# Side products of an attention and expert block on TensorE: full-array products in four groups a tile, against four column tiles of 32 in eight groups

## The reference

```
mod = silu(c) @ wmod            -> sa, ca, ga, sb, cb, gb per batch (ga, gb kept at 0.25 or more in size)
h  = layernorm(x) * (1 + ca) + sa
x  = x + ga * attention(h)      # 16 heads of width 8; head h has its own 64 rows of the batch
h  = layernorm(x) * (1 + cb) + sb
x  = x + gb * experts(h)        # router softmax over 8 experts, top 2, each expert a 128 x 128 matrix
```

## Time and profile before

| | us | share of span |
|---|---|---|
| profiled execution | 547.3 | |
| its span | 545.5 | |
| PE busy (4112 instructions) | 524.4 | 96% |
| PE weight loads | 221.6 | 41% |
| ScalarE busy | 495.6 | 91% |
| VectorE busy | 359.5 | 66% |
| POOL busy | 215.2 | 39% |
| exponentials L596, 512 of them | 485.8 | |
| weighted sums L795, 2048 matmuls | 247.8 | |
| scores L777, 1024 matmuls | 130.9 | |
| experts L825, 230 matmuls | 75.4 | |

### The profile page before, as it was taken

How to read it: one execution, slowest core, us unless ns; L and a number is a source line. 1 busy time by engine, 2 the same in 40 slices (tenths; PEclk the granted TensorE clock), 3 DMA queues, 4 the chain that set the end, 5 groups by cost and what they waited for, 6 DMA issues and landing times.

```text
span 545.5 us, 14324 instructions
## 1 busy us (share of the span) xinstructions
PE 524.4 (96%) x4112; PEld 221.6 (41%) x4112; DVE 359.5 (66%) x1259; ACT 495.6 (91%) x574; POOL 215.2 (39%) x430
## 2 busy tenths in 40 slices
PE   8789889999999999999999999999999999999897
PEld 8623334334343433434343434343333434343336
DVE  4446367667867666777766667867666677656466
ACT  1479999899999999999999999999999999999985
POOL 1223333344443344444333444443343444432344
PEclk9999999999999999999999999999999999999999
DMA  4663333333333333323333333233333332333000
GB/s 111 165 177 84 96 85 99 98 96 76 74 82 89 100 99 95 84 68 83 86 96 100 99 87 77 75 82 91 100 99 95 78 75 80 90 100 104 20 21 20
DMA packets 83341, 48.23 MB, mean 88 GB/s; under 512 B 59608, under 2 KB 74084, under 8 KB 83300
## 3 DMA queue, kind: packets, MB, share of 16 engines
q1 hardware_dynamic: 68860, 43.30, 29.7%
q10 hardware_dynamic: 14440, 4.38, 4.4%
HBM read 32.78 MB, written 14.87 MB: 87 GB/s over the span
## 4 chain that ended last, share of the span: by engine, by line
PE 88%; ACT 8%; issue 1%; DVE 1%; DMA 0%; SPq 0%; POOL 0%; DVEq 0%; POOLq 0%; ACTq 0%
PE ps_attn L795 43%; PE ps_scores L777 22%; ACT probs L596 8%; PE ps_side L825 8%; PE ps_side L715 3%; PE ps_side L722 2%; PE ps_side L731 1%; PE ps_side L709 1%; PE ps_side L808 1%; PE ps_scores L664 1%; PE ps_side L812 1%; PE ps_scores L825 1%; PE ps_side L702 1%; DMA wqkv_in<-in_L_attn_Wqkv_dram 0%; PE ps_attn L668 0%
## 5 line engine op out<-in xcount | busy, mean ns | idle before, releaser
L596 ACT ACTIVATE probs<-ps_scores 128x1024 f32<-128x1024 f32 x512 | 485.8, 1028 | 38.4 <-PE ps_scores L777 30.3
L795 PE MATMUL ps_attn<-probs,values 128*32 128x512 f32 x2048 | 247.8, 602 | 0.0
L777 PE MATMUL ps_scores<-query_stack,key_stack 32*128 32x512 f32 x1024 | 130.9, 500 | 15.1 <-ACT probs L596 8.7
L777 PEld LDWEIGHTS ps_scores<-query_stack,key_stack 32*128 32x128 f32 x1024 | 49.4, 183 | 166.1 <-ACT probs L596 161.2
L451 POOL TENSOR_SCALAR var_eps<-moments 128x1 f32<-128x1 f32 x64 | 12.4, 194 | 223.0 <-DVE moments L1167 151.0
L795 PEld LDWEIGHTS ps_attn<-probs,values 128*32 128x32 f32 x2048 | 53.6, 109 | 108.8 <-issue 108.7
L825 PE MATMUL ps_side<-experts_gated,h2T 128*128 (+1 forms) x230 | 75.4, 410 | 0.0
L1163 DVE TENSOR_TENSOR x<-ps_side,x_gated 128x128 f32<-128x128 f32 x31 | 9.0, 292 | 63.3 <-PE ps_side L825 59.1
L1156 DVE RECIPROCAL sums_inv<-sums 128x128 f32<-128x128 f32 x31 | 29.5, 952 | 27.7 <-DMA attnT<-a_scr 27.7
L1240 DVE TENSOR_TENSOR weighted<-ps_side,coef 128x256 f32<-128x256 f32 x114 | 46.5, 408 | 1.1 <-PE ps_side L825 1.1
L500 POOL TENSOR_TENSOR mix<-weighted 128x512 f32<-128x512 f32 x29 | 37.1, 1281 | 4.0 <-ACT weighted L614 4.0
(11 more groups left out here) (170 smaller groups left out, 514.1 us busy)
## 6 DMA issues: line engine op xcount, KB each, us to landing
key_stack<-k_scr SPq DMA_DIRECT2D x128, 128.0 KB, 2.7
query_stack<-q_scr SPq DMA_DIRECT2D x125, 64.0 KB, 2.2
q_scr<-qk_parts SPq DMA_DIRECT2D x94, 64.0 KB, 1.7
k_scr<-qk_parts SPq DMA_DIRECT2D x64, 64.0 KB, 1.7
a_scr<-attn ACTq DMA_DIRECT2D x120, 18.0 KB
sums<-a_scr SPq DMA_DIRECT2D x31, 64.0 KB, 2.1
attnT<-a_scr SPq DMA_DIRECT2D x31, 64.0 KB, 2.2
out_dram<-out_all ACTq DMA_DIRECT2D x28, 64.0 KB, 1.8
```

What stands on the lines that cost most here:

```text
L596: nc.scalar.activation(probs[:, k % RING, g, :], ps_scores[:, slot(k, g), :], ACT.Exp, scale=SCALE)\
L777: mm = nc.tensor.matmul(out_, key_stack[p0:p0 + 32, parity, 2 * k:2 * k + 2, :].rearrange("p j r -> p (j r)"), query_stack[p0:p0 + 32, par ...
L795: mm = nc.tensor.matmul(ps_attn[q:q + 32, :], values[:, parity, g, k, :], probs[:, k % RING, g, h * HALF:(h + 1) * HALF], start=(k == 0), ...
```

## The change

Every side product in the tiles is made by `product`: four matmuls with 32 weight columns each, on the four column tiles, over the same moving columns. The transposes are then ordinary products with the identity. The start-up and the end of the kernel keep the whole array.

TensorE's order becomes, for each key block k: scores of k, side group k, weighted sum of block k - 2. The four groups of experts are groups 1, 2, 5 and 7; a group waits for the emptying of the one before. VectorE's order follows. The experts are no longer gated ahead but the mix afterwards on POOL, except for the last batch (`experts_last`), and POOL copies the gated Wo of the batch to `wo_now`. The norm maximum becomes a flag for each row, and a product with ones counts the rows.

```diff
+            def product(dst, stationary, moving, whole):
+                if whole:
+                    return nc.tensor.matmul(dst, stationary, moving, start=True, stop=True)
+                for q in range(0, P, 32):
+                    mm = nc.tensor.matmul(dst[q:q + 32, :], stationary[:, q:q + 32], moving, start=True, stop=True, tile_position=(0, q))
+                return mm
+            def transposed(dst, src, whole):
+                return nc.tensor.transpose(dst, src, ident[:]) if whole else product(dst, src, ident[:], whole)
...
             def a_project_v(ps, u1, ring):
                 for n in range(G):
-                    for odd in range(2):
-                        mm = nc.tensor.matmul(ps[odd * R:(odd + 1) * R, n * R:(n + 1) * R],
...
+                    for q in range(0, P, 32):
+                        odd, r = q // R, n * R + q % R
+                        mm = nc.tensor.matmul(ps[q:q + 32, n * R:(n + 1) * R], hT[:, ring, r:r + 32],
+                                              wvT[:, odd].rearrange("p k d -> p (k d)"), start=True, stop=True, tile_position=(0, q))
...
-                nc.tensor.matmul(ps, norm_max[:].broadcast_to([P, P]), ident_r[:], start=True, stop=True).then_inc(ev["normT_done"], 1)
+            def a_flags(ps, u1):
+                reached(pe, ev["norm_flag_done"], u1)
+                nc.tensor.matmul(ps, ones_cols[:], norm_flag[:], start=True, stop=True, tile_position=(0, 0)).then_inc(ev["flags_done"], 1)
...
+            def side0(at, parity, before, after):
+                if before >= 4:
+                    reached(pe, weighted_done[1], at[-3])
...
+                if before >= 2:
+                    c_project(ps_side, at[-1])
                 if after >= 1:
+                    a_flags(ps_side[0:32, P + R:P + R + 1], at[2])
+            def emptied0(at, before, after):
+                if before >= 2:
+                    reached(pe, ev["x1_done"], at[-1])
                 if after >= 1:
+                    reached(pe, ev["bounded_done"], at[2])
+            def side1(at, parity, before, after):
+                if before >= 4:
+                    emptied0(at, before, after)
+                    c_experts(ps_side, experts_in, parity, 2)
+            def side2(at, parity, before, after):
+                if before >= 4:
                     reached(pe, weighted_done[2], at[-3])
+                    c_experts(ps_side, experts_in, parity, 3)
...
+            def side3(at, parity, before, after):
+                if before >= 4:
+                    reached(pe, weighted_done[3], at[-3])
...
+                    c_transpose(ps_side, at[-1])
                 if before >= 2 and after >= 1:
                     a_project_v(ps_side[:, P:2 * P], at[2], 1 - parity)
...
+            def side4(at, parity, before, after):
+                emptied3(at, before, after)      # h2T_done, values_done
                 if after >= 2:
                     a_project_qk(at[3], parity)
...
+            def side5(at, parity, before, after):
+                if before >= 3:
+                    emptied4(at, before, after)  # qkT_done
+                    c_experts(ps_side, experts_last if after == 0 else experts_in, 1 - parity, 0)
+            def side6(at, parity, before, after):
+                if before >= 3:
                     reached(pe, weighted_done[0], at[-2])
...
                 if after >= 3:
                     a_transpose(at[4])
+                if before >= 2 and after:
+                    c_logits(ps_side, at[-1], parity)
                 if after >= 2:
+                    a_norms(ps_side[:, P + NE:P + NE + 2 * J], at[3])
+            def side7(at, parity, before, after):
+                if before >= 3:
+                    if after >= 3:
+                        reached(pe, ev["hT_done"], at[4])
+                    if after >= 2:
+                        reached(pe, ev["norm_max_done"], at[3])
+                    if after:
+                        reached(pe, ev["logits0_done"], at[-1])
+                    c_experts(ps_side, experts_last if after == 0 else experts_in, 1 - parity, 1)
...
+                for k in range(KT):
                     with pe.If(flag == 0):
+                        if k == 0:
+                            exact_maxima(t, parity)
+                        scores(at[0], at[1], parity, k, True)
                     with pe.Else():
+                        if k == 0:
+                            pe.sem_inc(m_scores, M_PE)
+                        scores(at[0], at[1], parity, k, False)
...
+                    SIDES[k](at, parity, before, after)
+                    if k >= 2:
+                        weigh(at[0], at[1], parity, k - 2)
+                    elif before:
+                        weigh(at[-1], at[0], 1 - parity, KT - 2 + k)
```

Before, `c_weigh(.., 0)` stood directly behind `a_qk` and ahead of `a_qk_parts`, and `c_vals` ahead of `a_norm_max`. POOL's order: `gated_x` with the copy of Wo goes ahead of the `rstd` of the first norm, `mix_eight` behind the squares, and `mix_two` has one multiplication more:

```diff
+                g.tensor_tensor(mixed_gated[:], mixed[:], gate, ALU.mult).then_inc(ev["mixed_gated_done"], 1)
...
+                g.tensor_copy(wo_now[:], wo).then_inc(ev["wo_done"], 1)
```

More of the change, by code:

```diff
@@ L815, in c_experts @@
[L815 removed]
+                product(ps[:, P:P + NE], h2T[:, ring, :], routerT[:], whole).then_inc(ev["logits_done"], 1)
+            def c_experts(ps, weights, ring, piece, whole=False):
                 e0, e1 = PIECES[piece]
                 if piece == 0:
[L820 to L826 removed]
@@ L907, in side3, with tile @@
                 if after == 0:
-                    c_project(ps, at[0], (T - 2) // TB)
-            def counts(t, before):
+                    c_project(ps_side, at[0], wo_gated[:, (T - 2) // TB, :])
+            SIDES = (side0, side1, side2, side3, side4, side5, side6, side7)
+            def tile(t, parity, before, after):
                 at = {n: plus(pe, t, n) for n in range(-4, 5)}
-                batch = {n: batch_of(pe, at[-n]) for n in (2, 3, 4) if n <= before}
-                return at, batch
@@ L916, in between_sides @@
-            def between_sides(at, parity, before, k, exact):
-                scores(at[0], at[1], parity, k, exact)
-                for past_k in (k - 3, k - 2):
-                    if past_k >= 0:
-                        weigh(at[0], at[1], parity, past_k)
-                    elif before:
-                        weigh(at[-1], at[0], 1 - parity, KT + past_k)
-                if k + 1 < KT:
-                    scores(at[0], at[1], parity, k + 1, exact)
-            def tile(t, parity, before, after):
-                at, batch = counts(t, before)
@@ L1285, in weights_gated, with tile @@
                 assert step.n == SETUP_ALL
-            def tile(banks, t, parity, before, after, past):
+            def tile(t, parity, before, after):
                 at = {n: plus(dve, t, n) for n in range(-4, 5)}
@@ L1554, in _ @@
             prologue()
-            tiles(dve, lambda t, parity, before, after: tile([ps_side] * 4, t, parity, before, after, 0))
+            tiles(dve, tile)
             last()
```

348 lines of the change are left out of this document (145 added, 203 removed).

## The result

The changed kernel takes 575.25 us (574.58 to 575.76) beside 546.70 us for the kernel before on the same chip: ratio 1.0515, 95% interval 1.0498 to 1.0532. The forecast was 544.7 with a range of 527 to 558. It is slower by 5%, and outside the range.

The account below looks back on a forecast made before the run. TensorE was taken as the bound, ScalarE close behind; the change wins 1 us a tile on TensorE and loses it waiting on VectorE. Loop tiles +1.5, total -2.2: 547.3 to 545.1, less 0.4 for the median, 544.7 us; range 527 to 558.

Parts of the forecast that it names:

- Side 4 to side 6: TensorE's side product 6 waits for VectorE's weighing: 4.48 us against 3.72 for two free slots, 0.76 lost a tile.
- POOL's *new* operations: Copy of wo and gating of the mix on POOL, 0.2 and 0.46 us; uncovered, they would delay only the store.
- side 0 to 1: First slot of a tile on TensorE, waiting for x1, its statistics and the bounded flag: 1.77 us, not 1.71.
- sides 1 to 4: Three TensorE slots, each with scores, a side product and one weighted sum: 1.86 us each.
- side 6 to 7: Hand-over through norm maximum, shifted logits and the new flag operation: 1.93 us, of which 0.07 is lost.
- the seam: Between tiles, TensorE's sequencer tests the loop and waits for loads: 0.39 us exposed at the loop's end, nothing inside the body.
- the count of 24: TensorE's sequencer starts its between-tile steps with 24 loads and matmuls of the double weighted sum still queued.
- ScalarE's long idle time: Sign in the changed profile: ScalarE idles once a tile, not four times.
- A: Rival: VectorE's chain before side product 6 fits two slots; tiles 14.9 and 15.3 us, kernel 525 us; chance 0.22.
- B: Rival: TensorE's between-tile steps are exposed in full, 0.84 and 0.41 us; 13 us more, 558 us; chance 0.15.
- C: Rival: small matmuls in slot 6 each cost time, 0.75 us instead of 0.18; 16 us more, 560 us; chance 0.05.
- D: Rival: side products on column tiles do not run together, +1.3 us in four slots; over 650 us; chance 0.02.

Follow-up runs that it names:

- the head mended: On the kernel with POOL's mix additions early and the weighing ahead of the router's base: whole-array side products in tile 0 alone; 533.98 us, ratio 0.978.

## Why the prediction was wrong

**The step that failed** is the sum for "Side 4 to side 6". Its structure was right: this hand-over is the hard one, it comes once a tile, and VectorE's weighing releases it. Its terms were taken from the earlier trace rows as if an operation's mean were its own cost. They held waits for POOL, and the change moved the waits:

| term | taken | measured |
|---|---|---|
| qkT's end to the subtraction's end | 1.73 | 0.80 |
| xhat's end to bias_w's end | 0.28 | 1.73 |
| bias_w's end to base's end | 0.61 | 0.93 |
| side 4 to side 6 | 4.48 | 5.30 |

The first row gives back 0.93 us, the next two cost 1.77; the difference is the 0.82 by which the step was missed, but for 0.02 (the terms of the chain as the prediction lists them add up to 3.62 us, and it went on with 3.65). It priced POOL's *new* operations at nothing, "beside", and never asked what the *moved* ones lie over, though the change that it describes puts `mix_eight` behind the squares. Both sides of that were in the trace: the cast and the subtraction (0.87 and 0.91 us in the rows of one tile) lay under POOL's additions, and bias_w and base (0.16 and 0.37) lay free of them. The Trainium skill (SBUF — State Buffer, Who interferes with whom) states the rule: VectorE and POOL share one pair of ports, exclusively and for the whole instruction, and VectorE needs it for two inputs from SBUF or for its two-port modes. The runs here agree: pair_pw, bias_w, base, cast, subtraction and router_p wait to the end of POOL's operation, the weighing (one input in PSUM) and the reciprocals do not. One thing the runs set apart from it: POOL's 128x8 operations of the coefficients did not hold VectorE for their whole recorded length (in the kernel before, bias_w took 0.16 us at 316.47, in the middle of one from 316.43 to 316.84). Lost in the step were 1.58 us, where the prediction's upper bound was 1.1: its bounds held no wait for POOL at all.

That the wait is POOL's is shown three ways: with the additions held back bias_w falls from 1.03 to 0.16 us, with one addition 1.08 longer it grows by 1.07, and with the additions moved the wait goes to the operation that then lies under them. Part of the miss offset itself: that the cast and the subtraction would get 0.93 us cheaper was not foreseen either.

**In numbers.** The tile was 16.77 and not 15.81: 24 x 0.96 = 23.0 us of the 30.6 that were missed, most of it this one step (0.82 of the 0.96). Of the rest, 4.6 are in the tiles ahead of the loop (tile 0 was 20.7 us for an expected 18.4, tiles 1 and 2 16.45 and 15.60 for 14.7), 3.0 behind it, where tiles 28 and 29 have the same wait.

**What held.** The other slots: side 0 to 1 1.69 to 1.79 us (1.77 forecast), sides 1 to 4 1.86 to 1.90 each (1.86), side 6 to 7 2.01 (1.93), and the seam. The sequencer's header begins 0.1 us after side 7's first load. It stood at a wait just ahead of side 7 (stamped 305.99, the loads begin at 306.06), so this start says nothing of how much TensorE's queue holds, and the count of 24 on which the prediction rested it stays untested; the time came out as forecast, and TensorE's loads for the next scores wait 0.84 us in the body and 1.20 at the loop's end:

```profile
307.52 0.19 PEld L801 LDWEIGHTS ps_scores<-query_stack,key_stack 32*128 32x128 f32 x4 [0.84 <-ACT probs L608]
...
324.40 0.22 PEld L801 LDWEIGHTS ps_scores<-query_stack,key_stack 32*128 32x128 f32 x4 [1.20 <-ACT probs L608]
```

Side 7 to the next side 0 takes 1.89 us in the body and 2.27 at the loop's end: 0 and 0.38 exposed, for 0 and 0.39. ScalarE's long idle time comes once a tile, as forecast, and it is 1.5 us; 0.47 us more stand at the loop's end.

**The rivals.** A (the hand-over hidden) was false for this kernel. The experiments brought about its condition and one of its two tiles: with a step of 3.75 the tiles take 15.24 and 15.32, for A's 14.9 and 15.3, and with the head mended the kernel takes 534 for A's 525. In the body's tile 0.18 us stand between side 3 and side 4 (2.05 us for 1.87) and 0.1 between side 0 and side 1. B is false by the rows above. C is false: the 24 small matmuls of side 6 start within 0.19 us (320.81 to 320.99), for 0.18 in the sum and 0.75 in C. D is false: the four column tiles of the experts start within 0.02 us of each other, and the next four 0.24 us later. None of the rivals had POOL in it, so the range could not hold the time.

**What stays open.** That the long branch in the head waits for code is shown only in so far as it is gone with fewer instructions ahead of it. Tile 1's low clock goes along with that branch: in the eight kernels where it took 2.6 to 4.2 us the granted clock from 42 to 50 us is 0.62 to 0.86, and in the six without it is 1.00. Tile 0's clock (0.50 to 0.72 from 20 to 30 us in six of the kernels, 1.00 in the others) is not explained. What holds side 4 back by 0.18 us in the body's tile once the additions are early was not looked for, and which place of TensorE's loop is the good one was not worked out.

## What to carry to other kernels

Before an operation's mean is put into a sum, look at what the neighbour engine did at that moment, and at its time without it: the shortest of the group, or another line of the same shape. When an edit moves a large POOL operation, list what VectorE will run under it; one-element operations in a dependent chain are the worst to hit (0.16 us became 1.21). Column tiles for side products gained nothing here until, spread over the slots, they took switches of shape out of the tile. The kernels with the instructions that they add had a long branch in the unrolled head and, with four tiles in the loop, at the jump back.

## What the runs showed of the hardware that was not expected

- A VectorE addition of 128x1 elements takes 0.16 us alone and 2.28 under a POOL addition of 2.35.
- The wait for POOL falls on VectorE's single-input operations too, short and long: a 128x256 cast 0.29 and 0.88, a 128x8 tensor-scalar 0.23 and 0.66, xhat 0.34 and 2.38.
- A loop body of four tiles makes TensorE's jump back 3.9 us; of two tiles, 0.2.
- Eight fulfilled waits ahead of a loop move the late instructions at its end (0.19 us between the third and fourth load of the scores becomes 0.20 between the first and second), and change a pair of tiles by only 0.07 us.
- With whole side products in eight slots TensorE switches between rows, columns and the whole array 24 times a tile, with column tiles 16 times, and the tile takes 16.48 us against 15.47.
